# A graph network's edge loop: four edge streams turned in 32x32 squares by VectorE, gathers that add to rows of products, end rows found by search

## What is computed

```python
h = relu(layernorm(x)) @ enc_node_w + enc_node_b
e = edge_attr @ enc_edge_w + enc_edge_b
# per layer, z = h in the first, relu(layernorm(h)) in the others
msg = relu(z[src] + e) + EPS_MSG
m = msg * t
ex = exp(m - segment_max(m, dst)[dst])
agg = segment_sum(msg * ex / (segment_sum(ex, dst)[dst] + 1e-16), dst)
out = z + agg
conv = relu(layernorm(out @ w1 + b1)) @ w2 + b2
h = conv in the first layer, h + conv in the others
```

## Time and profile before

| | us |
|---|---|
| runs, median of 3 | 10204.41 (10202.23 to 10206.61) |
| profiled execution, its own time | 10274.8 |
| its span, first to last instruction | 10272.7 |
| GpSimd busy | 6401.6 |
| VectorE busy | 5354.4 |
| TensorE matmul busy | 4152.7 |
| ScalarE busy | 2811.0 |

### The profile page before, as it was taken

How to read it: one execution, slowest core, us unless ns; L and a number is a source line. 1 busy time by engine, 2 the same in 40 slices (tenths; PEclk the granted TensorE clock), 3 DMA queues, 4 the chain that set the end, 5 groups by cost and what they waited for, 6 DMA issues and landing times.

```text
span 10272.7 us, 64326 instructions
## 1 busy us (share of the span) xinstructions
PE 4152.7 (40%) x14287; PEld 2600.4 (25%) x14287; DVE 5354.4 (52%) x6544; ACT 2811.0 (27%) x5249; POOL 6401.6 (62%) x6648
## 2 busy tenths in 40 slices
PE   4444444443444443434334344343433344343443
PEld 3222222222222222222222222222222222222222
DVE  5666666664445545545345455454534454554544
ACT  2222222222222222222222222222222222222222
POOL 5767777664466666666456666666636666666662
PEclk7555555555555555555555555555555555555555
DMA  3333333332233333333223333333323333333331
GB/s 92 103 99 102 100 101 101 102 99 71 68 101 103 102 101 101 106 98 105 64 75 102 101 103 102 100 106 98 105 55 84 101 104 102 101 106 97 105 101 54
DMA packets 416899, 982.49 MB, mean 96 GB/s; under 512 B 153238, under 2 KB 154146, under 8 KB 364898
## 3 DMA queue, kind: packets, MB, share of 16 engines
q1 hardware_dynamic: 204258, 757.59, 19.9%
q0 software_dynamic: 212608, 224.56, 15.2%
HBM read 547.99 MB, written 433.68 MB: 96 GB/s over the span
## 4 chain that ended last, share of the span: by engine, by line
POOL 27%; another core or an unknown queue 23%; issue 22%; DVE 19%; PE 7%; ACT 1%; DMA 1%; DVEq 0%; POOLq 0%; ACTq 0%; SPq 0%
POOL gathered L411 27%; DVE maxima L794 5%; DVE run_num L811 4%; DVE psum L786 3%; DVE wmsg L805 3%; PE psum L483 2%; PE psum L481 1%; DVE one_hot L742 1%; PE psum L538 1%; PE psum L521 1%; DVE psum L916 1%; DMA gathered<-node_table,idx_s 0%; DVE one_hot_hi L745 0%; PE psum L513 0%
## 5 line engine op out<-in xcount | busy, mean ns | idle before, releaser
L411 POOL DMA_INDIRECT gathered<-node_table,idx_s x6448 | 6216.4, 964 | 3561.7 <-issue 2302.1
L786 DVE TENSOR_SCALAR psum<-psum,floor_col,t_col 128x512 f32<-128x512 f32 x808 | 661.3, 818 | 4266.0 <-remote 3284.2
L481 PE MATMUL psum<-cst,gathered 128*128 128x128 f32 x3232 | 960.0, 432 | 2834.5 <-DVE wmsg L805 1255.0
L608 ACT ACTIVATE psum<-psum 128x512 f32<-128x512 f32 x808 | 470.3, 582 | 5539.4 <-issue 2748.4
L463 PE MATMUL psum<-cst,run_den 128*128 128x128 f32 x3232 | 853.0, 415 | 2747.6 <-ACT rows_out L601 2141.3
L483 PE MATMUL psum<-attr_s,edgew_s 128*128 128x512 f32 x1616 | 1541.6, 1058 | 0.0
L463 PEld LDWEIGHTS psum<-cst,run_den 128*128 128x128 f32 x3232 | 590.3, 219 | 3653.9 <-issue 2888.4
L481 PEld LDWEIGHTS psum<-cst,gathered 128*128 128x128 f32 x3232 | 553.0, 212 | 3191.1 <-issue 2519.7
L601 ACT ACTIVATE rows_out<-psum 128x1024 f32<-128x1024 f32 x808 | 822.5, 1018 | 1285.6 <-remote 1239.3
L794 DVE TENSOR_TENSOR_SCAN maxima<-psum,maxima,reset_s 128x512 f32<-128x512 f32 x808 | 1037.5, 1284 | 53.9 <-issue 0.5
L809 DVE TENSOR_TENSOR_SCAN run_den<-psum,run_den,weight 128x512 f32<-128x512 f32 x808 | 1028.8, 1273 | 0.0
(11 more groups left out here) (140 smaller groups left out, 1651.6 us busy)
## 6 DMA issues: line engine op xcount, KB each, us to landing
edge_state<-rows_out SPq DMA_DIRECT2D x404, 1024.0 KB
attr_s<-in_attr SPq DMA_DIRECT2D x406, 512.0 KB
reset_s<-resets SPq DMA_DIRECT2D x406, 256.0 KB
gathered<-node_table,idx_s POOLq DMA_INDIRECT x6448
node_table<-tab SPq DMA_DIRECT2D x27, 224.0 KB, 2.2
arena<-edge_state,end_i POOLq DMA_INDIRECT x196, 2.5
x_s<-in_x SPq DMA_DIRECT2D x1, 1568.0 KB, 6.8
out_nodes<-arena SPq DMA_DIRECT2D x1, 1568.0 KB, 5.1
```

Source lines behind the costliest of these rows:

```text
L411: pool.indirect_dma_start(gathered[s][:, C * at:C * at + C], None, table, bass.IndirectOffsetOnAxis(ap=idx_s[i // 2][:, TPC * s + at:TPC * ...
L481: pe.matmul(sums[s][:, P * b:P * b + P], gathered[s][:, P * b:P * b + P], ident, is_transpose=True, start=(b == 0), stop=False, skip_group ...
L786: v.tensor_scalar(logit[s], sums[s], floor_col[:, :], t_col[:, :], ALU.max, ALU.mult).then_inc(logit_done, 1)
```

## The change

**Streams.** The edges are cut into four quarters instead of two halves, every second one backwards. A quarter holds 32 partitions. A chunk is 256 edges of each stream, so still 1024 edges in 202 chunks. On the partitions of a stream lie 32 channels at a time; the 64 channels are two stretches `q` of the free dimension.

**Products as rows.** In layer 0 TensorE forms the attribute products with the edges on the partitions (`products`), ScalarE copies them out of PSUM (`copy_products`), and SyncE stores them to `edge_rows` in DRAM, three pairs ahead of their use. Each layer loads them, 512 KB a pair, into `edges[u]`, and the gathers on GpSimd add the table rows to them in place (`compute_op=ALU.add`). The gathers of a pair wait for `edges_in`; they no longer wait for `x_done`.

**Turning.** VectorE turns `edges` into channels by partition with one transpose in squares of 32x32 (`turn_edges`, 512 columns), and the running sums back into rows with another (`turn_sums`, 1024 columns) straight into `rows_out`. TensorE has nothing in the loops of layers 1 to 3; ScalarE does not evacuate any more. ScalarE makes the messages (relu with a bias per partition, two steps of 256 columns) and the logits (one step of 512). The floor-and-scale step of VectorE goes. Every scan is now two of 256 columns: six scans a chunk instead of three.

**End rows.** The histogram, its one-hot tiles on VectorE and its matmuls go. Instead, at the start, for each of 49 tiles of nodes and two more targets, VectorE counts how many of 403 blocks of 512 edges end at or below the node (`find_blocks`), GpSimd gathers that block's ids (256 KB in one indirect gather), and VectorE counts within it (`count_in_blocks`); this runs between the steps of the node encoding. Some 40 small steps then form the rows.

**Merging.** Nodes that lie across a border of quarters are merged from six pieces, for three target rows. The messages and maxima of 64 partitions are stored in every pair (two transfers of 256 KB), and after the loop GpSimd fetches the needed ones with four small gathers and two more of stored rows before the merge.

The diff, cut to its core (lines with "..." stand for what is left out):

```diff
-N = 512
-TPH = N // P
-TPC = 2 * TPH
+STREAMS = 4
+LANES = 32
+N = 256
+W = 2 * N
+BLOCKS = N // LANES
 CHUNKS = 202
 PAIRS = CHUNKS // 2
+N2 = 2 * N
+W2 = 2 * W
 
 
...
+            def store_products(m, u):
+                sp.wait_ge(product_copied, 2 * m + 2)
+                sp.dma_start(edge_rows[m], made_s[u][:, :]).then_inc(product_out[u], 16)
+
+            def load_edges(m, u):
+                sp.dma_start(edges[u][:, :], edge_rows[m]).then_inc(edges_in[u], 16)
...
+                def pair(n, m, j, u):
+                    known = isinstance(j, int)
+                    after = u if known and m + 2 >= PAIRS else m + 2
+                    if isinstance(layer, int):
+                        if not known or m + LEAD < PAIRS:
+                            store_products(m + LEAD, 1 - u)
+                        if not known or m + LEAD + 2 < PAIRS:
+                            load_attr(m + LEAD + 2, 1 - u)
+                    sp.wait_ge(turn_done, n + 2)
+                    if isinstance(layer, int) and not (known and m + 2 >= PAIRS):
+                        sp.wait_ge(product_out[u], 16 * (j + 2))
+                    load_edges(after, u)
+                    sp.wait_ge(message_done, n + 2)
+                    sp.dma_start(head_msg_v[m], message[u][LANES:LANES + HEADS, :]).then_inc(msg_stored[u], 16)
+                    sp.wait_ge(scanned, n + 2)
                     load_resets(after, u)
-                    if not (isinstance(k, int) and k == 1):
-                        store_rows(n - 2, pair - 1, 1 - u)
-                    if last:
-                        store_rows(n, pair, u)
-
...
+            for t in range(SEEK):
+                hold(pool, pool_passed, block_found, t // GROUP + 1)
+                hold(pool, pool_passed, counted, t - GROUP + 1)
+                pool.indirect_dma_start(
+                    found_rows[t % GROUP], None, dst_blocks,
+                    bass.IndirectOffsetOnAxis(ap=block_i[:, t:t + 1], axis=0)).then_inc(block_in[t % GROUP], 16)
...
-                    s = i % 2
-                    if s == 0:
-                        wait(pool, x_done, n - 1)
-                    else:
-                        hold(pool, pool_passed, x_done, n - 1)
-                    if s == 0:
-                        hold(pool, pool_passed, idx_ready, PAIRS * layer + (2 if isinstance(k, int) and k == 0 else 2 * j + i // 2 + 1))
-                    for b in range(TPH):
-                        part = gathered_a if b < TPH // 2 else gathered_b
-                        for half in range(2):
-                            if half == 1 and isinstance(k, int) and k == 0:
-                                continue
-                            at = 2 * b + half
-                            pool.indirect_dma_start(
-                                gathered[s][:, C * at:C * at + C], None, table,
-                                bass.IndirectOffsetOnAxis(ap=idx_s[i // 2][:, TPC * s + at:TPC * s + at + 1], axis=0)).then_inc(part[s], 16)
+                    u, st = i // 2, i % 2
+                    if st == 0:
+                        hold(pool, pool_passed, idx_ready, PAIRS * layer + (2 if isinstance(k, int) and k == 0 else 2 * j + u + 1))
+                        hold(pool, pool_passed, edges_in[u], 16 * (pairs_before(layer, j, u) + 1))
+                    for b in range(BLOCKS):
+                        at = W * st + C * b
+                        col = BLOCKS * st + b
+                        pool.indirect_dma_start(
+                            edges[u][:, at:at + C], None, table,
+                            bass.IndirectOffsetOnAxis(ap=idx_s[u][:, col:col + 1], axis=0),
+                            compute_op=ALU.add).then_inc(gathered[i], 16)
 
...
+                for i, values in enumerate((head_msg, head_max)):
+                    for q in range(2):
+                        pool.indirect_dma_start(
+                            head_parts[:, 2 * i + q:2 * i + q + 1], None, values,
+                            bass.IndirectOffsetOnAxis(ap=head_i[0:HEADS, q:q + 1], axis=0)).then_inc(heads_in, 16)
                 for u in range(2):
                     hold(pool, pool_passed, rows_stored[u], 16 * SLOT_PAIRS[u] * (layer + 1))
-                hold(pool, pool_passed, empty_out, 16 * (layer + 1))
+                for i in range(2):
+                    pool.indirect_dma_start(
+                        head_rows[:, C2 * i:C2 * i + C2], None, state[0:EDGE_ROWS, :],
+                        bass.IndirectOffsetOnAxis(ap=head_row_i[0:TARGETS, i:i + 1], axis=0)).then_inc(heads_in, 16)
+                hold(pool, pool_passed, empty_out, 16)
                 if isinstance(layer, int):
...
+            def products(n, j, u, st):
+                if st == 0:
+                    pe.wait_ge(attr_in[u], 16 * (j + 1))
+                wait(pe, product_copied, n)
+                for b in range(BLOCKS // 2):
+                    at = W * st + P * b
+                    last = pe.matmul(made_ps[:, P * b:P * b + P], attr_s[u][:, at:at + P], edgew_s[:, :], start=True, stop=True)
+                last.then_inc(product_done, 1)
...
-                    for part in range(2):
-                        pe.wait_ge((gathered_a, gathered_b)[part][s], count)
-                        for b in (2 * part, 2 * part + 1):
-                            pe.matmul(sums[s][:, P * b:P * b + P], gathered[s][:, P * b:P * b + P], ident,
-                                      is_transpose=True, start=(b == 0), stop=False, skip_group_check=True)
-                    pe.matmul(sums[s], edgew_s[:, :], attr_s[u][:, at:at + N], start=False, stop=True,
-                              skip_group_check=True).then_inc(x_done, 1)
-                    if isinstance(layer, int):
-                        if not isinstance(n, int) or n >= 1:
-                            histogram(n - 1, 1 - s)
-                    if not (isinstance(k, int) and k < 2):
-                        out_rows(n - 2, s)
-                    if last_chunk:
-                        out_rows(n - 1, 1 - s)
...
+                def messages(n, j, i):
+                    s, u, st = i % 2, i // 2, i % 2
+                    act.wait_ge(turn_done, n + 1)
+                    wait(act, weighted, n - 3)
+                    if st == 0:
+                        wait(act, msg_stored[u], 16 * pairs_before(layer, j, u))
+                    for q in range(2):
+                        at = N2 * q + N * st
+                        last = act.activation(message[u][:, at:at + N], turned[s][:, N * q:N * q + N], ACT.Relu,
+                                              bias=bias_col[:, q:q + 1])
+                    last.then_inc(message_done, 1)
+                    act.wait_ge(message_done, n + 1)
+                    act.activation(halves(logit[s]), halves(message[u][:, :])[:, :, N * st:N * st + N], ACT.Copy,
+                                   scale=t_col[:, :]).then_inc(logit_done, 1)
...
+            def find_blocks(group):
+                for t in group:
+                    v.wait_ge(seek_steps, 6 + max(t - 1, 0))
+                    v.tensor_scalar((norm, square_junk)[t % 2][:, 0:FIND_BLOCKS - 1], lasts, seek[:, t:t + 1], 0.0, ALU.is_le, ALU.add,
+                                    accum_out=found[:, 0, t:t + 1]).then_inc(seek_steps, 1)
+                v.wait_ge(seek_steps, 6 + group[-1] + 1)
+                v.tensor_copy(block_i[:, group[0]:group[-1] + 1], found[:, 0, group[0]:group[-1] + 1]).then_inc(block_found, 1)
+
+            def count_in_blocks(group):
+                for t in group:
+                    v.wait_ge(block_in[t % GROUP], 16 * (t // GROUP + 1))
+                    wait(v, counted, t - 1)
+                    v.tensor_scalar(run[0][:, FIND * (t % 2):FIND * (t % 2) + FIND], found_rows[t % GROUP], seek[:, t:t + 1], 0.0, ALU.is_le, ALU.add,
+                                    accum_out=found[:, 1, t:t + 1]).then_inc(counted, 1)
...
+                def turn_edges(n, j, i):
+                    s, u, st = i % 2, i // 2, i % 2
+                    v.wait_ge(gathered[i], 16 * BLOCKS * (pairs_before(layer, j, u) + 1))
+                    wait(v, message_done, n - 1)
+                    v.transpose(turned[s][:, :].rearrange("p (q b e) -> p b q e", q=2, e=LANES),
+                                edges[u][:, W * st:W * st + W]).then_inc(turn_done, 1)
...
+                    for q in range(2):
+                        at = RING * q + N * i
+                        last = v.tensor_tensor_scan(maxima[:, at + 1:at + 1 + N], logit[s][:, N * q:N * q + N],
+                                                    reset_s[u][:, N * st:N * st + N], maxima[:, at:at + 1], ALU.max, ALU.add)
+                    last.then_inc(scanned, 1)
...
+                def run_sums(n, i):
+                    s, u, st = i % 2, i // 2, i % 2
                     v.wait_ge(exps_done, n + 1)
-                    v.scalar_tensor_tensor(wmsg[:, :], sums[s], floor_col[:, :], weight[:, :], ALU.max,
```

(29 more changed lines are left out.)

727 lines of the change are left out of this document (428 added, 299 removed).

## The result

The changed kernel takes 13119.01 us (median of 4, 13116.82 to 13126.86) where the kernel before takes 10203.32 in the same comparison: a ratio of 1.2861 [1.2838, 1.2883], so 29% slower. The forecast was 9090 us.

What follows compares the result with a forecast made beforehand. GpSimd issuing gathers was taken as the bound. Start 120, gathers 8074, layer 0 waits 50 and node phases 910 gave a span of 9154 us, times 0.9931 = 9090 us; range 8950 to 11600.

Steps and rivals of the forecast that it cites:

- Gathers: GpSimd in the edge loops: 6464 adding gathers at 0.944 us, 1.249 from start to start, 8074 us.
- the sum: Whole kernel: start, gathers, layer 0 waits and node phases add up to a span of 9154 us.
- The first rival: GpSimd's gather instruction: adding is dearer to issue; 12150 us at half as long again, about 15100 at twice; chance 0.27.
- Do the stops go?: GpSimd at chunk starts: stops, 1223.7 us before, vanish; layers 1 to 3 without wait, layer 0 50 us.
- The stops stay: GpSimd at chunk starts: stops come from the gathers' own queue, so 1261 us come back, 10340 us; chance 0.04.
- The load ahead of a pair: Gathers waiting for `edges_in`: no wait in layers 1 to 3, 50 us in layer 0, hidden behind 20.0 us a pair.
- VectorE and ScalarE: Edge loops, per chunk: VectorE 7.7 us and ScalarE about 3.6, both hidden under 10.0 us of gathers.
- the rival with VectorE as the bound: Edge loops: VectorE takes 11.0 us a chunk and sets the pace, 9850 us; chance 0.08.
- that rival: DMA engines in the loops become the bound: 9 packets an engine and gather at 0.1175 us, 10600 us; chance 0.09.
- From span to median: Whole kernel: the span of 9154 us times 0.9931, the earlier ratio of median to profiled execution, gives 9090 us.
- Start and ends: Before the loops and after each layer: first table gather at 120 us, node phases 910 us together.

Runs made afterwards that it cites:

- e2: The kernel before with its gathers adding to what the buffer holds instead of overwriting it, nothing else changed: 12940.41 us.
- e18: The kernel before with a 512-column fill on GpSimd after each gather as a pause: 12171.83 us where the kernel before takes 10279.15.
- e10: The kernel before with four gather buffers in place of two: 11926.51 us, ratio 1.1606 to the kernel before.
- e1: The changed kernel with copying instead of adding gathers, so products are left out of the message: 10732.49 us, ratio 1.0523 to the kernel before.
- e11: The changed kernel with gathers copying into their own buffer and VectorE adding the rows to the products: 10588.17 us, ratio 1.0313 to the kernel before.
- e7: The changed kernel with copying gathers and head rows' stores cut from 64 rows to 1: 9528.5 us, ratio 1.0673 to the kernel before.
- e6: The kernel before with four gather buffers, where the kernel before takes 8928.58 us: 8921.7 us, ratio 0.9993.

## Why the prediction was wrong

**Gathers: the step that failed.** "The price thus follows the rows, not the bytes, and the rows stay 128. I take 0.944 us". It was 1.543. Two copying rows of equal price say what bytes cost and nothing of an added operand. 6464 x 0.599 us is 3872 us of the 13118.4 - 9154 = 3964 us by which the sum was short; 135 us more of waits in layer 0, 9 less at the start and 4 less in the node phases account for the rest within 30 us. The first rival named the place and the mechanism; its size, an instruction of 1.42 us at half as long again and 12150 us, fell 7% short, and the range ended at an instruction of 1.33 us.

By the Trainium skill, "DMA: Bandwidth & Descriptors", section on the anatomy of one DMA on the GpSimd path, the prediction reasoned, the addition would cost next to nothing. That is not borne out here: 9 packets an engine and gather instead of 2 come with 0.6 us more; the traces don't count descriptors. The rule of two read descriptors (the Trainium skill, "Collectives: The Full Stack", Part 3) points the right way, but a surcharge of 0.47 us at 3 rows is mostly not a price by the row; the runs show that it is paid and not which part of the instruction pays it.

**Do the stops go?** They went, but not for the reason given. The prediction put them down to two buffers and a late word of TensorE. e2 and e18 keep both buffers and TensorE's word and have no such stops; e10 has four buffers and stops for longer. They go when the gathers come at 1.65 us or slower. At the forecast's price they would have stayed in another place: the frame with a copying gather takes 10732 us (e1) and 10588 (e11) on such chips, not 9090. The rival "The stops stay" at 10340 us (chance 0.04) was nearer there. Of its reason, one half holds (not TensorE's word and the two buffers); for the other half, the gathers' own queue, the runs show only that the gathers' pace decides: in e2 that queue carries 4.4 times the packets and nothing stops. Against it the prediction argued that GpSimd goes on with `x_done`; that told which semaphore ended the wait and not what made it late.

**The load ahead of a pair.** No wait in layers 1 to 3, as said; in layer 0 184.6 us for the 50 taken, although each pair there had 29.5 us of gathers and not 20 to hide it. With the 20 us of the forecast this term would have failed by more: 591.1 us in e7. So even at the forecast's gather, without late words and with smaller stores of head rows, the frame takes 9528.5 us and not 9090. The prediction had said that each wait in SP's order ends before the next load is due; in layer 0 of e7 SP waits 98 times, 2097.1 us in all and up to 34.9, for ScalarE's copy of the products, and the load stands behind that.

**VectorE and ScalarE.** The turn 0.711 (0.70 forecast), the turn of sums 1.219 (1.24), short scans 0.721 to 0.723 (0.72), difference 0.667 and weighted message 0.686 (0.70). ScalarE's message of 256 columns took 0.500, not 0.36, and logits 0.692. All hidden, as said; the rival with VectorE as the bound is out.

**DMA engines.** Nine packets an engine and gather, as that rival had it: 941936 / 16 / 6464 = 9.1 with the other groups' few. But a packet takes 0.194 x 16 x 13118 / 941936 = 0.043 us, not 0.1175, so the engines are 40% busy in the loops of layers 1 to 3.

**From span to median.** The factor 0.9931 has no ground in the runs. The changed kernel's profiled span is 13118.4 us and its median 13119.01. The 0.7% of before lies between comparisons, 10,200 us in two and 10,275 to 10,279 in two others. It was 63 us of the sum.

**Start and ends.** 111 us for 120, node phases 906 us for 910. The 906 hold four late words of some 38 us each, as the node phases of the kernel before do.

## What to carry to other kernels

Before a DMA's work is enlarged by an operand, time that one form by itself: a row of the same instruction without it doesn't bound it, and on an engine that sets the pace 0.6 us an instruction outweighs every engine relieved. Where the bound is the engine that issues the gathers, let an engine with slack do the addition: VectorE's cost 0.697 us a chunk, the gathers' 8 x 0.6 = 4.8. And a stop at a wait isn't healed by more buffers until it is known what makes the word late: here they turned 10,275 us into 11,927. Last, time the kernel before again beside each new form: it moved by 15% between comparisons.

## What the runs showed that was not expected

The adding indirect gather costs 1.54 to 1.56 us against 0.944 to 0.987 for 128 rows, 1.31 to 1.35 against 0.87 to 0.88 at 3 to 32; type conversion and bytes a row are free. On some chips words between TensorE, VectorE and ScalarE, and of VectorE to itself, come late while copying gathers follow at 1.25 us, by nearly 10 us at the earlier trace rows and by 34 us behind TensorE's turning in the node phase, and not at 1.65; in the trace of e6, on another chip, none is late at 1.25. The kernel before takes 10,200 to 10,279 us on the former and 8928 in the two comparisons on the latter (1.14 to 1.15 times). The changed kernel ran on the former alone, 13115 to 13125 us; on the latter it wasn't measured. An estimate is 4 x (126.5 - 88.8) = 151 us less, GpSimd's longest waits at a layer's end in it and in e7: some 12,970 us, a ratio of 1.45.
